# Block turns by VectorE and an exchange through DRAM in place of TensorE turns, in the cross attention of a gated two-layer kernel

## What is computed

```python
x = x + tanh(g_xattn[0]) * autocorrelation(layernorm(x), ctx, ctx)        # 8 heads, FFT, top 9 lags
x = x + tanh(g_ffn[0])   * lora_moe(layernorm(x), ...)                    # base product, routed LoRA
x = x + tanh(g_xattn[1]) * cross_attention(layernorm(x), ctx, mask, ...)  # 32 heads, 8 key heads, width 128
x = x + tanh(g_ffn[1])   * lora_sum(layernorm(x), ...)                    # product with folded weights
```

```python
q = layernorm(x) @ Wq.T      # 4 query heads of width 128 per key head
k, v = ctx @ Wk.T, ctx @ Wv.T
q, k = rmsnorm(q) * q_norm_w, rmsnorm(k) * k_norm_w
probs = softmax(q @ k.T / sqrt(128) + mask)
x += gate * (probs @ v) @ Wo.T
```

## Time and profile before

| | |
|---|---|
| median of 3 runs | 789.96 us |
| the profiled execution | 791.35 us |
| its span, first to last instruction | 789.6 us |
| TensorE matmul | 773.5 us, 98% of the span |
| TensorE weight load | 635.0 us, 80% |
| VectorE | 559.5 us, 71% |
| ScalarE | 414.7 us, 53% |
| GpSimd | 365.8 us, 46% |
| mean granted clock | 0.998 of full |

### The profile page before, as it was taken

One profiled execution on the slowest core, in us unless ns is written; L12 is line 12 of the kernel. 1 busy time (PEld: TensorE's weight loads), 2 busy tenths in 40 slices (PEclk: granted clock), 3 DMA queues, 4 the chain that ended last, 5 costly groups with the idle time before them and its releaser, 6 DMA issues.

```text
span 789.6 us, 13246 instructions
## 1 busy us (share of the span) xinstructions
PE 773.5 (98%) x4260; PEld 635.0 (80%) x4260; DVE 559.5 (71%) x1235; ACT 414.7 (53%) x1158; POOL 365.8 (46%) x429
## 2 busy tenths in 40 slices
PE   8899999989999999999999999999999999999998
PEld 5555665778888888888888888888888888788776
DVE  5888886667766766777777776676677777667874
ACT  5566654565456545654655555555555654355421
POOL 1668856564246324632553364336433533254532
PEclk9999999999999999999999999999999999999999
DMA  8311012021003100300031012002100201000011
GB/s 295 129 41 41 15 50 98 1 94 29 14 1 107 28 1 1 108 28 1 3 107 27 1 32 87 18 1 73 49 14 1 81 1 54 1 15 1 1 40 68
DMA packets 17124, 34.63 MB, mean 44 GB/s; under 512 B 2336, under 2 KB 2592, under 8 KB 16800
## 3 DMA queue, kind: packets, MB, share of 16 engines
q1 hardware_dynamic: 17056, 33.78, 13.5%
HBM read 31.67 MB, written 2.10 MB: 43 GB/s over the span
## 4 chain that ended last, share of the span: by engine, by line
PE 77%; DVE 8%; POOL 7%; issue 5%; ACT 1%; DMA 1%; SPq 0%; POOLq 0%; DVEq 0%; ACTq 0%
PE pair L862 18%; PE pair L863 18%; PE pair L864 18%; PE pair L964 4%; PE pair L977 3%; PE pair L1026 3%; PE pair L902 3%; POOL qkr L526 2%; PE pair L876 2%; POOL probn L518 2%; PE pair L966 1%; POOL wo_lo L512 1%; DVE xres L1325 1%; DVE score L1342 1%; PE pair L919 1%
## 5 line engine op out<-in xcount | busy, mean ns | idle before, releaser
L518 POOL TENSOR_TENSOR probn<-prob,erec 128x512 f32<-128x512 f32 x64 | 66.8, 1044 | 169.5 <-DVE erec L1357 169.5
L1381 DVE TENSOR_TENSOR qkn<-pair,qkr 128x640 f32<-128x640 f32 x64 | 52.8, 824 | 91.6 <-POOL qkr L526 91.6
L1362 DVE TENSOR_REDUCE qkss<-qksq 128x5 f32<-128x640 f32 x64 | 52.6, 821 | 84.4 <-ACT qksq L720 84.4
L713 ACT ACTIVATE prob<-score,nmax 128x128 f32<-128x128 f32 x256 | 99.6, 393 | 21.0 <-DVE nmax L1344 19.2
L702 ACT ACTIVATE oT_hi<-pair 128x512 fp32r<-128x512 f32 x64 | 38.1, 595 | 136.2 <-PE pair L864 136.2
L862 PE MATMUL pair<-wq_hi,nT_hi 128*128 128x512 f32 x256 | 106.6, 416 | 0.0
L862 PE MATMUL pair<-wo_hi,oT_hi 128*128 128x512 f32 x256 | 100.9, 394 | 2.8 <-issue 2.8
L864 PE MATMUL pair<-wq_hi,nT_lo 128*128 128x512 f32 x256 | 101.0, 394 | 0.0
L863 PE MATMUL pair<-wq_lo,nT_hi 128*128 128x512 f32 x256 | 100.9, 394 | 0.0
L863 PE MATMUL pair<-wo_lo,oT_hi 128*128 128x512 f32 x256 | 100.4, 392 | 0.0
L864 PE MATMUL pair<-wo_hi,oT_lo 128*128 128x512 f32 x256 | 99.8, 390 | 0.0
(11 more groups left out here) (178 smaller groups left out, 1985.0 us busy)
## 6 DMA issues: line engine op xcount, KB each, us to landing
wq_raw<-in_wq SPq DMA_DIRECT2D x32, 256.0 KB, 3.1
wo_raw<-in_wo SPq DMA_DIRECT2D x32, 256.0 KB, 2.9
wkv_raw<-in_wkv SPq DMA_DIRECT2D x8, 512.0 KB, 4.8
ctxn<-in_ctx_n SPq DMA_DIRECT2D x8, 256.0 KB, 3.6
ctxt<-in_ctx_t SPq DMA_DIRECT2D x8, 256.0 KB, 2.7
out<-wkv_raw SPq DMA_DIRECT2D x8, 256.0 KB, 2.0
xres<-in_x SPq DMA_DIRECT2D x1, 1280.0 KB, 8.3
wbase<-in_wbase SPq DMA_DIRECT2D x1, 1024.0 KB, 7.5
```

The source lines that it names most:

```text
L518: pool.tensor_tensor(probn[:], prob[:], erec[:].unsqueeze(2).broadcast_to([P, HG, P]), ALU.mult).then_inc(normed, 1)
L713: t = act.activation(prob[:, h, :], score[:, h, :], ACT.Exp, bias=nmax[:, h:h + 1], accum_out=esum[:, h:h + 1])
L1362: dve.tensor_reduce(qkss[:], qksq[:], AX.X, ALU.add).then_inc(qk_ss, 1)
L1381: dve.tensor_tensor(qkn[:], qk_bank, qkr[:].unsqueeze(2).broadcast_to([P, HG + 1, P]), ALU.mult).then_inc(qk_nat, 1)
```

## The change

The turning of queries, keys and probabilities leaves TensorE. VectorE turns 32x32 blocks within its own 32 partitions (`dve.transpose`), and writes them so that each partition holds, one after the other, the pieces for four groups of 32 destination partitions. SP writes these rows in one transfer to a scratch tensor in DRAM (`write_rows`) and reads them back in four, one for each group of 32 destination partitions (`read_blocks`), in pieces of 640 bytes (queries and key) or 512 bytes (probabilities). Two scratch tensors of each kind alternate.

With that go these edits:

- Scores are four plain float32 matmuls of 128x128 straight from the read tile, with no high and low halves. ScalarE scales the key only. The rows of the score tile are ordered otherwise (each block holds 32 tokens of all four heads), and the mask is laid out to match, 128x512, over constants of the first phase.
- The scores take one PSUM bank and not two; the projections alternate between two PSUM pairs from unit 3 on, so that a projection need not wait for the one before.
- `norm_probs` works in place, at the start of the next slot. Probabilities times values and output projection of unit n stand in slot n + 3.
- The slots of the weights' halves, of the folded weights and of the last phase move, and SP's weight loads stand between exchanges in a written order.

```diff
+BL = P // 32
-    WQ_AT = {2: (0,), 3: (1,), 4: (2,), 5: (3,)}
+    WKV_AT, WO_AT = 0, 3
+    WQ_AT = {1: (0,), 2: (1,), 4: (2,), 5: (3,)}
-    STAT, NORM, TURN, FEED = N - B + 3, N - B + 4, N - B + 5, N - B + 6
+    STAT, BIAS, TURN, FEED = N - B + 4, N - B + 5, N - B + 5, N - B + 6
...
@@ SyncE
+                def write_rows(n, tile, dram, turned, read, done):
+                    sp.wait_ge(turned, n + 1)
+                    if n >= 2:
+                        sp.wait_ge(read[n % 2], BL * landed(n - 2))
+                    sp.dma_start(dram[n % 2].rearrange("i z j r -> (i z) (j r)"), tile[:]).then_inc(done[n % 2], 16)
+                def read_blocks(n, tile, dram, written, done):
+                    sp.wait_ge(written[n % 2], landed(n))
+                    q = P // BL
+                    for j in range(BL):
+                        sp.dma_start(tile[j * q:(j + 1) * q, :].rearrange("z (i r) -> z i r", i=BL),
+                                     dram[n % 2][:, :, j, :].rearrange("i z r -> z i r")).then_inc(done[n % 2], 16)
...
+                def read_qk(n):
+                    need(sp, s_done, n - 1)
+                def read_probs(n):
+                    need(sp, p_h, n)
+                    need(sp, p_l, n)
...
+                for n in range(-1, N + 1):
+                    if on(n + 1):
+                        write_qk(n + 1)
+                    if n < 2 and on(n + 1):
+                        read_qk(n + 1)
+                    if on(n - 1):
+                        write_probs(n - 1)
+                    if n >= 2 and on(n + 1):
+                        read_qk(n + 1)
+                    if on(n - 1):
+                        read_probs(n - 1)
@@ VectorE
-                    dve.tensor_tensor(score[:], s_bank[:, :, 0, :], score[:], ALU.add).then_inc(masked, 1)
...
+                def turn_probs(n):
+                    need(dve, normed, n + 1)
+                    if n > 0:
+                        dve.wait_ge(p_out[(n - 1) % 2], landed(n - 1))
+                    dve.transpose(p_blocks[:].rearrange("p (j i y) -> p i j y", j=BL, i=BL),
+                                  prob[:].rearrange("p i (j z) -> p i j z", j=BL)).then_inc(p_turned, 1)
...
+                def turn_qk(n):
+                    need(dve, qk_nat, n + 1)
+                    if n > 0:
+                        dve.wait_ge(qk_out[(n - 1) % 2], landed(n - 1))
+                    dve.transpose(qk_blocks[:].rearrange("p (j h y) -> p h j y", j=BL, h=HG + 1),
+                                  qkn[:].rearrange("p h (j z) -> p h j z", j=BL)).then_inc(qk_turned, 1)
@@ ScalarE
-                def high_qk(n):
+                def scale_keys(n):
+                    act.wait_ge(qk_in[n % 2], BL * landed(n))
@@ TensorE
-                    for h in range(HG):
-                        pe.matmul(s_bank[:, h, :, :].rearrange("p i t -> p (i t)"), qT_hi[:, w],
-                                  kT[:].rearrange("p i t -> p (i t)"), start=True, stop=True, skip_group_check=True)
-                        t = pe.matmul(s_bank[:, h, 0, :], qT_lo[:, w], kT[:, 0, :], start=False, stop=True,
+                    for i in range(BL):
+                        t = pe.matmul(s_bank[:, i, :], queries(n, i), kT[:], start=True, stop=True,
...
                 def slot(n):
+                    if on(n - 3):
+                        probs_v(n - 3)
...
+                    if on(n + 2):
+                        project_qkv(n + 2)
+                    if batch(n, FEED) is not None:
+                        feed_forward(batch(n, FEED))
+                    if batch(n, TURN) is not None:
+                        turn_batch(batch(n, TURN))
+                    if on(n):
+                        scores(n)
...
+                    if on(n - 3):
+                        project_out(n - 3)
```

More of the change, by code:

```diff
@@ L344, in chunk @@
             return n - first if 0 <= n - first < CH else None
-        def turning(n):
-            return batch(n, TURN) or None
         def at(n):
@@ L357, in slots, with landed @@
                 slot(n)
+        def landed(n):
+            return 16 * (n // 2 + 1)
         with nc.Block() as block:
@@ L568, in slot @@
                             low_wq(g + 1, c)
+                    if n == 1:
+                        g_scale(B - 1)
+                    if n == 3:
+                        low_rows(B - 1)
+                    if on(n) and n > B and n % B == WO_AT:
+                        for h in range(HG):
+                            low_wo(g, h)
+                    if on(n + 2):
+                        inverse_norms(n + 2)
+                    if n == 2:
+                        for h in range(HG):
+                            low_wo(0, h)
                     c = chunk(n, FOLD + 2)
@@ L1194, in _ @@
                 routed_product(6)
-                turn_qk(0)
                 project_q(1, range(CH))
@@ L1207, in _ @@
                 project_kv(2).then_inc(qkv_done, 1)
+                scores(0)
                 slots(slot)
@@ L1326, in add_out @@
                                              ALU.mult, ALU.add).then_inc(y_add, 1)
-                    if batch(n + 3, STAT) is not None:
+                    if batch(n + 4, STAT) is not None:
                         k = b % 2
```

397 lines of the change are left out of this document (183 added, 214 removed).

## The result

The changed kernel took 741.75 us (median of four runs, 741.37 to 743.14), the kernel before in the same sessions 790.86: ratio 0.9383, 95% interval 0.9362 to 0.9404. The forecast was 737 us with a range of 726 to 764. The profiled execution took 742.11 us with a span of 740.3. The forecast span was 736.9.

The account below looks back on a forecast made before the run. TensorE was taken to bound the kernel. Span 789.6 - 58.9 (turns) + 1.9 (scores) + 2.0 (start) + 2.3 (end) = 736.9 us; 738.6 as profiled execution, 1.4 less for the median: 737 us, range 726 to 764.

Parts of the forecast that it names:

- TensorE is the bound and loses its turns: Middle slots: TensorE stays the bound, slot 9.49 to 8.60 us, gain 57.0 us; 72% chance.
- VectorE's turns: VectorE per slot: two block turns, 0.75 us for 128x640 and 0.60 for 128x512; cover remains even if they cost double.
- Rival 2: Middle slots: VectorE becomes the bound if turns take 2.0 and 2.4 us; 49 us back, 786 us; 6% chance.
- Packets: DMA engines, exchange pieces and rows: 0.05 us each, 5.1 us a slot, plus 1.1 for weights.
- Rival 3: DMA engines full if small pieces cost as much as 2 KB ones: 10.1 us a slot, 829 us; 9% chance.
- The exchange has room: Probabilities' loop over two slots: a slot can't be shorter than 7.1 us, under TensorE's 8.60, with E at 6.1.
- E: Time from the end of the probabilities' block turn to their last block landed: counted 6.1 us, estimated 6 to 8.
- threshold of 9.1: Value of E in us below which TensorE's 8.60 us slot stays longer; at 10.9 the exchange eats the whole gain.
- rival 1: Middle slots: the exchange ends last in part, E 9.1 to 10.9, slot 8.6 to 9.5 us; 766 us; 13% chance.
- Weights: Output weights' low halves on GpSimd: 0 to 0.5 us in seven places, taken as 0; SyncE's loads covered by slack.
- The start: First probabilities' exchange: a tie at 13.4 us, but output weights' halves delay the second slot; +2 us, 0 to 6.
- The end: Last two batch turns, right before their feed-forward, cost 1.6 us each; a 0.89 us wait goes; net +2.3 us.

Follow-up runs that it names:

- e1: Changed kernel with nine 128x128 turns of a constant put back on TensorE in each of slots 3 to 55; 788.48 us, ratio 0.9976.
- e6: Kernel before with only the scores in plain f32, no low halves of queries and keys, turns still on TensorE; 787.68 us, ratio 0.9968.
- e8: Changed kernel with SyncE reading the probabilities' blocks ahead of the queries' and keys' blocks from slot n = 2 on; 797.61 us, ratio 1.0093.
- e9: Changed kernel with four unawaited 4-byte transfers issued by SyncE ahead of the probabilities' reads in slots 3 to 55; 788.69 us, ratio 0.9969.
- e2: Changed kernel with each block read split in two, sixteen reads per slot instead of eight, same bytes; 935.04 us, ratio 1.1814.
- e11: e7 with weight loads issued between the blocks' writes and reads, and output weight loads spread over four slots; 738.25 us, ratio 0.9333.
- e7: Changed kernel with SyncE, in slot n = 1 only, writing the probabilities ahead of reading unit 2's queries and keys; 740.5 us, ratio 0.9365.
- e4: Changed kernel with the first output weights' halves and row statistics moved earlier on ScalarE and GpSimd at the start; 743.48 us, ratio 0.9399.
- e3: Changed kernel with each batch's turn and its halves moved ahead of other work in the last slots; 741.01 us, ratio 0.9386.
- e12: e11 with the end order of e3 added; 737.57 us, ratio 0.9319.

## Why the prediction held, and where its steps were off

**TensorE is the bound and loses its turns: right, and shown** (e1, which gives the turns back and loses the gain). The term was mis-sized: 57.0 us foreseen, 65.3 measured. The forecast put the scores at 0.90 us by the earlier trace rows; they take 0.81 where a split matmul follows. In e6, where f32 turns follow, the same scores take 0.88 (408.43 to 409.31), and so nothing was gained there. The rest of the slot took 7.66, not 7.70.

**VectorE's turns: right in kind, a little small.** 845 and 711 ns, against 750 and 600 taken, 0.2 us a slot. The estimate of 1.24 and 1.56 us, worked out from "VectorE: DVE Perf Modes", "The three transpose paths" in the Trainium skill, was far too high. In f32 a block turn costs about what any pass of its size costs here (824 for the multiply of 128x640). One pass grew unforeseen: the probabilities' low half reads SBUF alone now, and takes up to 1.86 us where a GpSimd pass is under way, as at 451.56; by the mean, 842 ns, it costs 0.16 us a slot over the like pass of 681. The Trainium skill, "SBUF — State Buffer", section "SBUF: two separate sides", says that a VectorE pass with two SBUF inputs and a GpSimd pass that reads SBUF lock each other out for a whole instruction. The trace agrees: 1.78 us is one pass and up to one of GpSimd's (5.48 / 4 = 1.37) ahead of it, all 22 long ones begin beside a GpSimd pass, and where VectorE came first it was GpSimd's pass that grew, from 1.30 us to as much as 1.74. Rival 2 was out: DVE at 78%.

**Packets: the share was right, the price a little high.** The DMA share is 0.57, 4.8 us of a slot, where 5.1 was taken (1280 x 0.05 / 16 = 4.0, and 1.1 for the weights, which the forecast's words name once more beside the 5.1). The 0.05 us stood for each piece and row of the exchange. The pieces took 0.028 and 0.042 us and the rows 0.1, so the exchange comes to 3.9 us a slot, the forecast's own case of pieces that cost by their bytes (3.8). That the mean of all packets, 0.052, is near the 0.05 is chance. Rival 3 was out, and with it the 11 us a slot estimated from the Trainium skill's "DMA: Bandwidth & Descriptors" ("Rules for kernel authors", "Bandwidth"): the four reads of probabilities, issued within 1.8 us to disjoint partitions, each landed in 2.0 us. Only the writes show something like it: in the changed kernel's own trace they land in 3.2 and 3.4 us where they are issued 0.47 us apart, and in 2.4 and 2.1 where over 1.5 us lie between them.

**The exchange has room: the weakest step.** The forecast said E of 6.1, estimated 6 to 8, against a threshold of 9.1. Measured are 8.3 to the last landing and 8.4 to ScalarE's copy on the average, and single ones of 10 to 12.5. Two things failed. The count let SyncE issue the four query reads, 1.8 us, while the probabilities' write was landing, so that the reads of probabilities went out 2.5 us after the block turn. But each read waits for its own write, and the queries' write goes out only 0.47 us ahead of the other: SyncE stood for 275.78 - 272.88 = 2.9 us and then issued the query reads, and the reads of probabilities came 4.75 us behind their write. And the exchange was counted along itself, with SyncE's ten issues as 4.4 us of 8.60, not as a round. SyncE's row holds the wait for the write to land as well: two writes and their landing (3.4), eight reads (3.7) and a weight load (0.5) are 7.6 us of 8.47, and 10 with four output weight loads. A round of 10 is caught up in the next ones at 0.9 us each, and so single exchanges over the threshold of 9.1 cost little. e8 and e9 show how narrow that was: rival 1, at 766, was right in kind about what lies next, but it underpriced it: +56 us for the reads' order (clock included), +47 for four issues. What e2 and e9 added to the round, 3.5 and 1.2 us, came out in the slot for the most part: 3.3 and 0.8 us over the changed kernel's 8.6. In e2 the round decides, since SyncE waits for nobody any more, and in e9 nearly so. For e8 it is not shown: there the keys come late, and SyncE itself waits.

**Weights: 0 foreseen, 6.1 us measured** (51 slots from unit 5 on take 437.83 us, 51 x 8.466 is 431.77; before, 51 of 9.487 left nothing over). About half is GpSimd's low halves of the output weights, 0.5 us in each of six slots, "0 to 0.5" in the forecast. In e11's trace it stands in the output projection, 3.32 us there against 2.81. The other half, 2.9 us, is what e11 took away.

**The start: +2 foreseen, range 0 to 6.** TensorE's idle time from 138 to 205 us rose from 67.00 - 64.00 = 3.0 to 8.65 us: +5.7. The count called it a tie at E = 6.1; E was 10.2 there, since SyncE read unit 2's queries and keys ahead of writing the first probabilities (write issued at 158.29, block turn done at 155.37). Some 1.3 us of the 10.2 is one late landing, since other runs of this order have 8.5 to 8.8. e7, with 7.1, shows no gap on TensorE that runs of the old order do not show as well. So E at the start was longer than counted for the reason given, but what holds the gaps is open; e4 shows only that they move between slots.

**The end: +2.3 foreseen.** What is left of the 16.0 us is 16.0 - 6.1 - 5.7 = 4.2, a remainder and not a measurement of its own. The two gaps are at the foreseen place, with 2.68 and 2.53 us in place of 1.6. But e3 and e12, which put the turns of the batches earlier, gain nothing: the waits stand elsewhere in the last slots then. What bounds these is open.

The sum: 8.3 us too little gained in the slots, 6.1 + 3.7 + 1.9 = 11.7 too little charged, so the span came out 3.4 us over the forecast. That the 737 us came so near is luck: two errors of 8 and 12 us cancelled.

## What to carry to other kernels

Where work moves from a busy engine to transfers, write down the issuing queue's round as you would an engine's: every issue, and every landing it stands still for. If it comes within some 10% of the slot, as here, put the issues that nobody awaits (weights, stores) into the landing wait, and read first what the consumers' rows ask for first. Where TensorE begins to wait, look at the granted clock before pricing the wait: part of it may be the clock's. Then test the margin by adding a few idle issues before trusting it. And a plain "engine X is 96% busy" says nothing of how near the next bound is; the shares of the chain did.

## What the runs showed of the hardware that was not expected

- Two writes of 320 and 256 KB issued 0.47 us apart land in 3.2 and 3.4 us, issued over 1.5 us apart in 2.4 and 2.1 (the changed kernel), in 2.2 and 2.1 in e11. Behind four 256 KB loads they land in 5.7 and 5.9 (issued at 262.45 and 262.92). So a queue that is late makes itself later.
- An issue by SyncE took 0.43 us, but 26 of 624 between 200 and 690 us took 0.6 to 1.8 us in the changed kernel, 21 us in all beyond the usual price. The other runs with the exchange have 18 to 23 of these, the kernel before none in 53. No run tells why.
- A packet took time about by its bytes: 0.028 us at 512, 0.042 at 640, 0.099 at 2,048, 0.103 at 2,560 bytes (means of the changed kernel).
- Four transfers of 4 bytes, which move next to nothing, still cost 1.17 us of queue time in a row, 0.29 each against 0.47 for one of 64 KB, and 47 us over 53 slots.
- A VectorE subtraction with both operands in SBUF takes 682 ns by the median, and up to 1.86 us when it begins beside a GpSimd pass over SBUF, while the like pass that reads PSUM (L1415) stays between 657 and 692 ns.
- A block turn in f32 on VectorE: 711 ns for 128x512, 845 for 128x640, about what a plain pass of the size takes (681 to 742, and 824).
- Four f32 score matmuls occupy TensorE for 0.81 us ahead of a split matmul and 0.88 ahead of f32 turns.
